# Routed block of layer 0: its weights loaded during the attention ahead of it, and its router weighed on the raw rows there

## The reference, cut to what matters

```python
x = x + jnp.tanh(g_xattn[0]) * _L0_xattn_ref(_layernorm(x, axis=-1), ctx_1024, ctx_1024, mask, wq, wk, wv, wo, bo)
x = x + jnp.tanh(g_ffn[0]) * _L0_ffn_ref(_layernorm(x, axis=-1), attention_mask, position_ids, router_w, router_b, ...)

def _layernorm(x, axis=-1, eps=1e-05):
    m = jnp.mean(x, axis=axis, keepdims=True)
    v = jnp.var(x, axis=axis, keepdims=True)
    return (x - m) / jnp.sqrt(v + eps)

def _L0_ffn_ref(x, attention_mask, position_ids, router_w, router_b, wq, wk, wv, wo, w1, w2, ln1, ln2):
    weights = (x @ router_w)[..., 0] + router_b[0]          # 16 x 128
    k = int(0.125 * s)                                      # 16
    topv, topi = jax.lax.top_k(weights, k)
    sel_mask = weights > topv[:, -1][:, None]
    sel_idx = jnp.sort(topi[:, :k - 1], axis=1)             # 15 rows of each batch
    x_sel = x[bidx, sel_idx]
    ...                                                     # attention and a gelu MLP on the 15 rows
    proc = x2 * w_sel[..., None]
    out = jnp.zeros_like(x).at[bidx, sel_idx].set(proc)
    return out + x * (1.0 - sel_mask)[..., None]
```

## Time and profile before

| what | us |
|---|---|
| median of 3 runs | 1597.31 |
| lowest and highest | 1595.0 and 1604.65 |
| span of the profiled execution, first to last instruction | 1600.8 |
| first attention, to the barrier | 0 to 195.8 |
| first phase of the routed block | 195.8 to 216.4 |

### The profile page before, as it was taken

One profiled execution on the slowest core, in us unless ns is written; L12 is line 12 of the kernel. 1 busy time (PEld: TensorE's weight loads), 2 busy tenths in 40 slices (PEclk: granted clock), 3 DMA queues, 4 the chain that ended last, 5 costly groups with the idle time before them and its releaser, 6 DMA issues. The chain is left out here.

```text
span 1600.8 us, 31601 instructions
## 1 busy us (share of the span) xinstructions
PE 1386.6 (87%) x10662; PEld 1150.0 (72%) x10662; DVE 953.2 (60%) x2331; ACT 664.8 (42%) x1313; POOL 422.6 (26%) x578
## 2 busy tenths in 40 slices
PE   8999878889999994999999998999999997401588
PEld 5888645677799983788888887779999996400245
DVE  4888665666422225777777774832222265688887
ACT  3666453420344430333333334335555522430277
POOL 1000000012122210122221221246666633421141
PEclk9999999899799997999999998889999999755799
DMA  3000020673111107111111202012333344421001
GB/s 107 21 20 15 6 92 1 218 268 61 60 34 41 34 22 226 62 51 49 49 47 32 44 1 93 1 52 92 92 93 93 86 173 134 108 19 10 1 14 40
DMA packets 105328, 106.53 MB, mean 67 GB/s; under 512 B 36080, under 2 KB 92160, under 8 KB 105088
## 3 DMA queue, kind: packets, MB, share of 16 engines
q1 hardware_dynamic: 89312, 70.91, 14.6%
q0 software_dynamic: 11136, 28.93, 6.6%
q10 hardware_dynamic: 4768, 5.25, 1.1%
HBM read 83.19 MB, written 20.71 MB: 65 GB/s over the span
## 5 line engine op out<-in xcount | busy, mean ns | idle before, releaser
L3598 PEld LDWEIGHTS L2f_bank<-L2f_xT,L2f_w_tile 128*128 128x128 f32 x1264 | 154.5, 193 | 7.4 <-ACT L2f_xT L3662 3.4
L3598 PE MATMUL L2f_bank<-L2f_xT,L2f_w_tile 128*128 128x128 f32 x1264 | 155.2, 276 | 3.0 <-ACT L2f_xT L3662 3.0
L785 POOL TENSOR_TENSOR L2x_probs<-L2x_probs,L2x_inv_sum 128x512 f32<-128x512 f32 x64 | 66.3, 1057 | 268.4 <-DVE L2x_inv_sum L1062 268.4
L3712 DVE TENSOR_TENSOR L2f_hT<-L2f_gate_h,L2f_bank 128x256 f32<-128x256 f32 x79 | 33.3, 421 | 148.5 <-ACT L2f_gate_h L3669 148.5
L3521 POOL DMA_INDIRECT L2f_y_rows<-L2f_xn,L2f_put_row x79 | 78.2, 989 | 55.2 <-DVE L2f_xn L3728 51.6
L3656 ACT COPY L2f_w_tile<-L2f_w_up 128x1024 f32 x79 | 82.7, 1046 | 17.4 <-issue 17.4
L3513 POOL DMA_INDIRECT L2f_rows<-L2f_x_rows,L2f_take_row x79 | 77.0, 975 | 44.7 <-DVE L2f_take_row L3496 21.3
L3598 PEld LDWEIGHTS L1f_bank<-L1f_xT,L1f_w_tile 128*128 128x128 f32 x736 | 85.6, 192 | 1.1
L3598 PE MATMUL L1f_bank<-L1f_xT,L1f_w_tile 128*128 128x128 f32 x736 | 85.9, 275 | 0.0
L3615 PE MATMUL L1f_bank<-L1f_w_down,L1f_hT 128*128 x368 | 83.1, 379 | 0.0
L3615 PE MATMUL L2f_bank<-L2f_w_down,L2f_hT 128*128 x316 | 81.4, 380 | 0.1
(11 more groups left out here) (677 smaller groups left out, 3321.2 us busy)
## 6 DMA issues: line engine op xcount, KB each, us to landing
L1f_w_up<-in_L_ffn_w SPq DMA_DIRECT2D x16, 512.0 KB, 8.2
L1f_w_down<-in_L_ffn_w SPq DMA_DIRECT2D x16, 512.0 KB, 9.0
L2f_got<-L2f_y_rows SPq DMA_DIRECT2D x16, 512.0 KB, 4.4
L2f_w_up<-in_L_ffn_gate_w SPq DMA_DIRECT2D x16, 256.0 KB, 2.9
L2f_w_up<-in_L_ffn_up_w SPq DMA_DIRECT2D x16, 256.0 KB, 3.0
L2f_w_down<-in_L_ffn_down_w SPq DMA_DIRECT2D x16, 256.0 KB, 3.6
x<-in_x SPq DMA_DIRECT2D x4, 512.0 KB, 7.9
L0x_ctx<-in_ctx SPq DMA_DIRECT2D x16, 128.0 KB, 2.1
```

The costliest lines, as they stand in the source:

```text
L785: nc.gpsimd.tensor_tensor(probs[c][:, :, :], probs[c][:, :, :], inv_sum[:, c, :][:, :, None].to_broadcast([P, 4, P]), ALU.mult).then_inc(s ...
L3598: x = nc.tensor.matmul(products(j, m), w_tile[j][:, at:at + P], xT[j][:, k * P:(k + 1) * P], start=(k == 0), stop=(k == KT - 1))
L3712: nc.vector.tensor_tensor(hT[j][:, 0:F], gate_h[j][:, 0:F], bank[2 + j][:, F:2 * F], ALU.mult).then_inc(q["h"], 1)
```

## The change

The tiles that the routed block loads, and `weight`, move into a class `DepthLoads` that is made before the attention. SP issues the twelve DMAs inside the attention, behind the loads of batches 2 and 3 and ahead of the loop over the others, and waits for them at the attention's end.

The product with the router's row is taken in the attention, in `update`, right behind the statistics, on the row of x as it then is, not normalised (`weigh`). As the normalised row is x times `rstd` plus `neg_mean_rstd`, the product with it is the raw product times `rstd`, plus `neg_mean_rstd` times the sum of the router's row. So the block needs three operations on 128 x 16 (lines 1320 to 1323) and the sum, `router_sum`, taken once in the attention's tail. ACT still writes `x_aug`; nobody needs it now before PE's gather, which waits for all 16 batches of it. The 11 idle products at the start become 4.

```diff
+class DepthLoads:
+    def __init__(self, core, stack):
...
+        self.sems = core.sems_in("depth", ["router", "weights", "weighed"])
+    def load(self, sp):
+        sp.dma_start(self.router_row[:, :], ins["L0_ffn_router_w"].rearrange("d a -> a d").to_broadcast([P, D])
+                     ).then_inc(s["router"], 16)
...
+    def all_in(self, sp):
+        sp.wait_ge(self.sems["weights"], 16 * 11)
+    def weigh(self, dve, j, b):
+        self.core.nc.vector.scalar_tensor_tensor(self.junk[j][:, :], cols(self.core.x, b * D, D), 1.0, self.router_row[:, :],
+                                                 ALU.mult, ALU.mult, accum_out=cols(self.weight, b, 1)
+                                                 ).then_inc(self.sems["weighed"], 1)

 narrow_attention, on SP:
-            with sp.Fori(1, B // 2) as i:
+            for j in range(2):
+                body(j, 2 + j)
+            depth.load(sp)
+            with sp.Fori(2, B // 2) as i:
                 for j in range(2):
                     body(j, i * 2 + j)
+            depth.all_in(sp)

 narrow_attention, on DVE:
                 dve.wait_ge(s["updated"], b + 1)
                 take_stats(core, b)
+                dve.wait_ge(depth.sems["router"], 16)
+                depth.weigh(dve, j, b)
...
             over_batches(dve, body)
-            update(B - 2)
+            update(0, B - 2)
+            sum_router()
             take_heads(1, B - 1)
-            update(B - 1)
+            update(1, B - 1)

 depth_routed_block, on SP: the twelve DMAs and the wait are gone

 depth_routed_block, on PE:
-            stay_warm(core, bank[7], 11)
+            stay_warm(core, bank[7], 4)
...
             pe.wait_ge(s["pick"], 1)
-            pe.wait_ge(s["mask_in"], 16)
...
             pe.wait_ge(s["aug"], 2)
+            pe.wait_ge(s["xn"], B)

 depth_routed_block, on DVE:
             finish_norm_vector(core, dve, s, temps)
             dve.sem_inc(s["normed"], 1)
+            nc.vector.tensor_tensor(weight[:, :], weight[:, :], core.rstd[:, :], ALU.mult)
+            link(nc.vector.tensor_scalar(mean_part[:, :], core.neg_mean_rstd[:, :], depth.router_sum[:, :],
+                                         depth.router_b[:, :], ALU.mult, ALU.add))
+            link(nc.vector.tensor_tensor(weight[:, :], weight[:, :], mean_part[:, :], ALU.add))
+            dve.sem_inc(s["weight"], 1)
             link(nc.vector.tensor_reduce(of_pair[:, :], ...))
             nc.vector.tensor_reduce(parity[:, :], ...)
-            dve.wait_ge(s["router"], 48)
-            for b in range(B):
-                dve.wait_ge(s["xn"], b + 1)
-                after(dve, s["weighed"], b - 1)
-                nc.vector.scalar_tensor_tensor(junk[b % 2][:, :], x_aug[:, b, 0:D], 1.0, router_row[:, :],
-                                               ALU.mult, ALU.mult, accum_out=cols(weight, b, 1)).then_inc(s["weighed"], 1)
-            dve.wait_ge(s["weighed"], B)
-            link(nc.vector.tensor_scalar(weight[:, :], weight[:, :], router_b[:, :], None, ALU.add))
-            dve.sem_inc(s["weight"], 1)
```

More of the change, by code:

```diff
@@ L289, in narrow_attention @@
+def narrow_attention(core, depth):
     nc, ins = core.nc, core.ins
@@ L609, in take_heads, with update @@
                                         ).then_inc(s["headsT"], 1)
-            def update(b):
+            def update(j, b):
                 dve.wait_ge(s["projected"], b + 1)
@@ L625, in body @@
                 if has_two_before(b):
-                    update(b - 2)
+                    update(j, b - 2)
                 shift(b, 1)
@@ L649, in _, with sum_router @@
                                     ).then_inc(s["gated_bias"], 1)
+            def sum_router():
+                nc.vector.tensor_reduce(depth.router_sum[:, :], depth.router_row[:, :], AX.X, ALU.add)
             over_batches(dve, body)
-            update(B - 2)
+            update(0, B - 2)
+            sum_router()
             take_heads(1, B - 1)
-            update(B - 1)
+            update(1, B - 1)
 def one(ap, b):
@@ L1125, in _, with depth_routed_block @@
             update(B - 1)
-def depth_routed_block(core):
+def depth_routed_block(core, depth):
     nc, ins = core.nc, core.ins
@@ L1148, in depth_routed_block @@
         sb = core.sbuf_in(ctx)
[L1149 to L1157, removed]
+        ln1, ln2, w4, w1, w2 = depth.ln1, depth.ln2, depth.w4, depth.w1, depth.w2
+        attn_mask, pos_in, weight = depth.attn_mask, depth.pos_in, depth.weight
+        mean_part = sb("mean_part", [P, B])
         temps = sb("L0f_temps", [P, 4, B])
@@ L1160, in depth_routed_block @@
         apart = sb("apart", [P, P])
-        weight = sb("weight", [P, B])
         unchosen = sb("unchosen", [P, B])
         x_aug = sb("x_aug", [P, B, XW])
-        junk = [sb(f"L0f_junk{j}", [P, D]) for j in range(2)]
         weight16 = [sb(f"weight16{j}", [B, P]) for j in range(2)]
@@ L1180, in depth_routed_block @@
         s = core.sems_in(tag, NORM_SEMS + [
-            "router", "weights", "small", "consts", "normed", "xn", "weighed", "step", "weight", "wT", "spread",
-            "placed", "pick", "aug", "U", "U_out", "pickT", "mask_in"])
+            "small", "consts", "normed", "xn", "step", "weight", "wT", "spread", "placed", "pick", "aug", "U", "U_out",
+            "pickT"])
         phases = Phases(nc)
         block = phases.open()
[L1188 to L1207, removed]
         @block.gpsimd
@@ L3788, in layer0 @@
         def layer0():
-            narrow_attention(core)
-            core.give_back_sems()
-            depth_routed_block(core)
+            with ExitStack() as pair:
+                depth = DepthLoads(core, pair)
+                narrow_attention(core, depth)
+                core.give_back_sems()
+                depth_routed_block(core, depth)
             core.give_back_sems()
```

30 lines of the change are left out of this document (29 added, 1 removed).

## The result

| kernel | median | lowest to highest | runs | ratio to before, 95% interval |
|---|---|---|---|---|
| before | 1599.67 us | 1595.0 to 1605.52 | 8 | |
| after | 1591.24 us | 1586.76 to 1601.64 | 8 | 0.9949 [0.9927, 0.9971] |

The kernel is 0.5% faster: by the ratio 8.2 us, with an interval from 4.6 to 11.7 us. The forecast was 1591 us and "within one per cent"; both hold. That the median of after lies within 0.2 us of the forecast is therefore luck. The eight runs a side tell 0.5% from no change, finer than the one per cent that the prediction took for the limit. The profiled execution of after took 1590.06 us.

The account below looks back on a forecast made before the run. PE paces the loop; the DVE's queue bounds the tail and its weighing chain the block's first phase. Tail 0.8 lost, block 6.7 gained, loop and loads nothing: 1597.3 - 5.9 = 1591.4 us, range 1584 to 1600.

Parts of the forecast that it names:

- The row gather starts at 205.8 in place of 212.53: Routed block's first phase: PE's row gather starts once ACT's last pass of `x_aug` reaches PE, 6.7 us gained.
- Behind it nothing changes: Routed block behind the row gather's start: no further change, so the 6.7 us gain carries through to the phase's end.
- the rival of the clock: Block's first phase: clock falls in PE's sparse stretch, 3.9 us of work takes up to twice as long, 1595.3; chance 0.18.
- the prediction's own signs of being wrong: PE idling behind the DVE in the loop, batch 4 waiting for its mask, or the phase's clock below 1.00.
- the 6.7 forecast: Block's first phase: row gather at 205.8 instead of 212.53, so 6.7 us gained.
- With 11 it would wait until 205.56: Block's start: with 11 idle products in place of four, the transpose would wait for them until 205.56.
- a cost of nothing out of 0.76 us of cover: Attention's loop: one weighing a batch, 0.35 to 0.51 us, is hidden by the DVE's 0.76 us idle time.
- 0.8 us for two weighings on the path: Attention's tail: weighings ahead of the last batch's reciprocal and behind the last statistics, 0.35 to 0.51 us each, 0.8 lost.
- The wait ahead of the weighings: Block's first phase: the DVE's weighing starts only at 200.80, put down to a wait for three DMAs.
- The parenthesis: Block's phase end: had only the weighing moved, the wait for loads until 213.6 or later would take most of the gain.
- the loads' 18 to 20 us: The twelve loads needed from 195.83 until 213.6 to 215.6 in before, 18 to 20 us with nothing beside them.
- the 5.9 forecast: Whole kernel: 0.8 us lost in the tail less 6.7 gained in the block, 5.9 us faster.

Follow-up runs that it names:

- loads only: Against before, only the twelve loads move into the attention; weighing, 11 idle products and bias stay in the block: 1599.23 us, ratio 1.0001.
- the kernel with 11: Against after, the idle products at the phase's start put back from 4 to 11: 1599.11 us, 0.9992 of before.
- the weighing alone: Against before, weighing moved into the attention with router's row, bias and positions; mask and eight weights still loaded in the block: 1592.46 us, ratio 0.9951.
- the two attempts: After with PE busier ahead of the gather, 0.9974 of before; the same with a third idle product in the second phase too, 0.9960.

## Why the prediction was right, and where a step was off

**The block: the mechanism was right, one duration was not.** "The row gather starts at 205.8 in place of 212.53" holds to the tenth, counted from the phase's start: 9.98 us behind it against the forecast 10, 16.65 before, and the releaser is ACT's last pass. (The phase itself started at 193.5, not at 196.6, by the tail's clock.) The step that was off is "Behind it nothing changes". I took 1.95 us for the gather from the one execution that I had. In the profiles of all nine changed kernels it takes 3.1 to 3.7 us, with 4 and with 11 idle products ahead of it. So the rival of the clock came true, at 1.64 us of its 3.9, and with it one of the prediction's own signs of being wrong: a clock below 1.00 in the phase. But as it fell in both other profiles with 11 products ahead, too, the fall belongs most likely to the kernel before as well, and its profile is the one that escaped; with one profile of before this isn't shown. Phase against phase, loads only (PE's order as in before) has 21.9 us and after 15.5: 6.4 us, near the 6.7 forecast, though neither end of it is the one that I read. The Trainium skill, page "TensorE: Matmul & The Clock Gate", Part 1, made idleness of PE the risk here; the rows agree that the clock falls in this sparse stretch (0.50 from 204 to 206). By that rule I feared for fewer idle products; the row of the kernel with 11 shows the same 0.50, so eleven are no safeguard. Whether fewer make the fall more frequent, one profile a kernel can't tell.

**The idle products: right, and bigger than said.** "With 11 it would wait until 205.56", 9.68 us behind the first product, was measured as 9.54 behind the phase's start. The consequence was in the text, the weight of it wasn't: put back, they take the whole gain as far as can be told, 0.0043 or 6.9 us against after (5.5 were expected, and the clock's earlier drop put the row gather 0.8 later than that).

**The loop: right.** The forecast was a cost of nothing out of 0.76 us of cover. Measured were 0.33 us of idle time used per batch, no change of the period, and 0.35 us once in the loop's first step, which the prediction didn't look at. The idle time left is 0.43 us a batch, not 0.3, as the accumulator's read overlaps the next instruction: both start at 186.37 in the tail. The doubled weighing shows that there was cover for two.

**The tail: half of what was forecast, overlaid by the clock.** The forecast had 0.8 us for two weighings on the path. The last one cost 0.34 to 0.41 us; the one ahead of the reciprocal lies behind 0.69 us of idle time that the DVE still had in the last batch's turn, and cost nothing. In this pair of profiles the tail's clock gave back more than that. It differs from profile to profile, among kernels with weighings too, and must not be counted.

**The loads: worth nothing, for a reason I had only half.** Moving them alone gave 1.0001. The wait ahead of the weighings, which the prediction put down to three DMAs, was indeed theirs, but ACT's pace was so close behind that it cost 0.2 us. The parenthesis, that a weighing moved alone would lose most of the gain to the loads, fell: it took the loads' 18 to 20 us as given, and they take some 15 without the three small ones.

**The sum.** Phase 6.4, less 0.35 in the loop and 0.34 to 0.41 in the tail, makes 5.6 to 5.7 us, by profiles, near the 5.9 forecast: the phase gave 0.3 less and the loop cost 0.35 more than forecast, and the tail cost 0.4 less. The ratio says 8.2 with an interval from 4.6, and the weighing alone 7.8 from 4.3. The two agree within the intervals. Whether the 2 us or so between are scatter, or later stages gain by starting earlier, stays open: after's lead grows there in the profile, but so does the lead of other kernels, and their clocks rise and fall in different places. Open as well is what holds the clock at the gather; the two attempts failed.

## What to carry to other kernels

A product that is linear in a normalised row can be taken ahead of the normalisation and mended on its small result, which takes it off the chain; then the filler put ahead of that chain has to be cut to the new, earlier event, or it eats the gain. Measure the slack that is to hide moved work by doubling the work, not by the idle time of one row alone; and don't expect time from loads that other work already hides, but look at which small ones stand at the head of their queue.

## What the runs showed that I had not expected

The clock at the row gather fell to 0.50 in nine profiles of ten, whether 9.68 or 3.67 us of idle products stood at the phase's start, and with one product more behind the transpose; the tenth, the one profile of before, has 9.68 us of them. Three loads of 0.14 MB, 688 of their 816 packets under 512 B, ahead of 3.7 MB delayed the last landing by some 3 us. A product with accumulator whose rows show 0.42 + 0.08 us costs 0.33 to 0.35 us of its queue when something follows at once.
